# First attention's softmax weights: the multiplication moved to GpSimd, one bounding step on VectorE, one step to bf16 on GpSimd

## The reference, cut to what matters

```python
def _fq(x, delta, zp, n_bits):
    xi = _round_ste(x / delta) + zp
    xq = jnp.clip(xi, 0.0, 2.0 ** n_bits - 1.0)
    return (xq - zp) * delta
...
sim = jnp.einsum('bhid,bhjd->bhij', _fq(q, dq, 128.0, 8), _fq(k, dk, 128.0, 8)) * SCALE
attn = jax.nn.softmax(sim, axis=-1)
out = jnp.einsum('bhij,bhjd->bhid', _fq(attn, dw, 0.0, 8), _fq(v, dv, 128.0, 8))
```

## Time and profile before

| | |
|---|---|
| time, median of 3 runs | 3125.79 us (3118.36 to 3126.36) |
| the profiled execution | 3128.91 us, span 3127.2 us |
| busy: TensorE, VectorE, ScalarE, GpSimd | 2520.2, 1899.8, 1297.8, 1023.1 us |
| mean granted TensorE clock | 0.843 |
| recurrence, about 2512 to 2766 us | 254 us |
| last attention, about 2766 to 3127 us | 361 us |

### The profile page before, as it was taken

The page is one execution under the profiler, slowest core; times in us unless marked ns, Lnnn a source line. Parts: engine busy times, 40 slices in busy tenths (PEclk is TensorE's granted clock), DMA queues, the critical chain, the costliest instruction groups (busy, mean ns, idle before and its releaser), DMA issues. The chain is left out here.

```text
span 3127.2 us, 47208 instructions
## 1 busy us (share of the span) xinstructions
PE 2520.2 (81%) x16568; PEld 1811.3 (58%) x16568; DVE 1899.8 (61%) x4639; ACT 1297.8 (42%) x3243; POOL 1023.1 (33%) x903
## 2 busy tenths in 40 slices
PE   4369888898888888898989898888888765448997
PEld 3247676666666766575767666666666442334443
DVE  4975666776766576868686767676764320004766
ACT  1534344545443345454444544344432211224654
POOL 3841132423242233343333334242321010005775
PEclk9679898898888989898989898979888765558999
DMA  4220011101111011111111111110110000001110
GB/s 187 45 52 10 20 18 24 38 21 21 31 31 24 18 28 31 31 25 27 35 24 29 30 24 28 23 28 22 28 25 7 5 18 23 0 0 34 35 37 22
DMA packets 222407, 90.45 MB, mean 29 GB/s; under 512 B 205280, under 2 KB 212784, under 8 KB 221424
## 3 DMA queue, kind: packets, MB, share of 16 engines
q1 hardware_dynamic: 215728, 67.68, 10.9%
q10 hardware_dynamic: 6464, 19.93, 1.7%
HBM read 27.80 MB, written 9.44 MB: 12 GB/s over the span
## 5 line engine op out<-in xcount | busy, mean ns | idle before, releaser
L775 POOL TENSOR_SCALAR work<-work 128x1024 bf16<-128x1024 f32 x128 | 466.6, 3650 | 319.4 <-DVE work L1285 260.6
L1002 PE MATMUL psum<-hT,w_l 128*128 128x256 f32 x2048 | 490.1, 397 | 19.2 <-ACT hT L1356 9.4
L1002 PEld LDWEIGHTS psum<-hT,w_l 128*128 128x128 f32 x2048 | 401.6, 199 | 90.5 <-ACT hT L1356 14.0
L734 POOL TENSOR_TENSOR rstd<-ms,half 128x2 f32<-128x2 f32 (+1 forms) x144 | 101.5, 706 | 850.1 <-DVE ms L1089 446.1
L1456 ACT ACTIVATE work<-psum 128x1024 f32<-128x1024 f32 (+1 forms) x224 | 222.0, 1021 | 284.9 <-PE psum L934 251.8
L1440 ACT ACTIVATE work<-psum,nbias,qs 128x256 f32<-128x256 f32 x512 | 281.6, 565 | 122.4 <-DVE nbias L1194 120.4
L827 PE MATMUL psum<-hT,w_l 128*128 128x256 f32 x896 | 249.4, 433 | 14.7 <-ACT hT L1356 13.5
L836 PE MATMUL psum<-w_l,xhat 128*128 128x256 f32 x640 | 198.2, 464 | 50.1 <-DVE xhat L1265 34.7
L1014 PE MATMUL psum<-w_l,work 128*128 128x256 f32 x1024 | 231.9, 385 | 2.4 <-DVE work L1318 2.1
L827 PEld LDWEIGHTS psum<-hT,w_l 128*128 128x128 f32 x896 | 189.7, 219 | 58.1 <-issue 18.7
L1356 ACT ACTIVATE hT<-psum,cols 128x256 f32<-128x256 f32 x256 | 121.9, 530 | 230.4 <-PE psum L818 229.3
(11 more groups left out here) (183 smaller groups left out, 4719.7 us busy)
## 6 DMA issues: line engine op xcount, KB each, us to landing
w_l<-in_w_l ACTq DMA_DIRECT2D x1, 5120.0 KB, 25.1
x_res<-in_x SPq DMA_DIRECT2D x16, 256.0 KB, 2.8
res<-x_res ACTq DMA_DIRECT2D x16, 256.0 KB, 2.4
w_l<-res SPq DMA_DIRECT2D x16, 256.0 KB, 2.8
out<-w_l ACTq DMA_DIRECT2D x16, 256.0 KB, 2.0
w_l<-in_w_l ACTq DMA_DIRECT2D x1, 3072.0 KB, 13.4
work<-work SPq DMA_TRANSPOSE x192, 3.1
w_l<-in_w_l SPq DMA_DIRECT2D x2, 1024.0 KB, 8.5
```

What stands on the lines that cost most here:

```text
L775: eng.tensor_scalar(rounded_part(a, u, i, p), e_part(a, u, i, p), MAGIC, -MAGIC, ALU.add, ALU.add) \
L1002: mm = eng.matmul(banks.tile(key)[:, h * TOKENS:(h + 1) * TOKENS], w1[:, k, h, m * P:(m + 1) * P], hT[p][:, k, :], start=(k == 0), stop=(k ...
```

## The change

In A1's rounds, VectorE's `probs` ends with `rsum`. GpSimd's `probs` multiplies the e slot's 4 x 256 columns by the broadcast `rsum`, in place. VectorE's `round_off`, until now only A2's, takes the minimum with 255 and adds MAGIC on all 1024 columns. GpSimd's new `whole` subtracts MAGIC, multiplies by 1.0 and writes bf16. The rounding is done by VectorE's addition of MAGIC now. The transposes, and the exponentials that take the slot again, wait for the new signal `whole_ready`.

The plan is given the new steps and other durations: A1's rounds get 0.6 (VectorE), 2.0 (GpSimd), 0.85 (VectorE), 1.2 (GpSimd) in place of 2.1 and 2.05; A2's rounding 1.15 in place of 1.0. A task can now have a `lag`, a time after its end before its followers start, which leaves its engine free: a transpose holds `sync` for 1.25 us and lands 2.0 later, and loads and stores have a lag of 2.0 in place of tasks on `clock`.

```diff
-TURN, LAND = 2.5, 2.5
+LAND = 2.0
...
-            rest[t] = self.us[t] + max([HOP + rest[f] for f in followers[t]], default=0.0)
+            rest[t] = self.us[t] + self.lag[t] + max([HOP + rest[f] for f in followers[t]], default=0.0)
...
-                    soonest[f] = max(end[b] + HOP * (b[0] != f[0]) for b in self.after[f])
+                    soonest[f] = max(end[b] + self.lag[b] + HOP * (b[0] != f[0]) for b in self.after[f])
...
-                e = work.add("vector", "probs", a, (u, i), p, 2.1 if a.self_attn else 1.4, e)
-                if not a.self_attn:
-                    e = work.add("pool", "probs", a, (u, i), p, 1.25, e)
-                e = work.add("pool" if a.self_attn else "vector", "round", a, (u, i), p, 2.05 if a.self_attn else 1.0, e,
-                             turned.get(2 * u + i - HELD))
+                e = work.add("vector", "probs", a, (u, i), p, 0.6 if a.self_attn else 1.4, e)
+                e = work.add("pool", "probs", a, (u, i), p, 2.0 if a.self_attn else 1.25, e)
+                e = work.add("vector", "round", a, (u, i), p, 0.85 if a.self_attn else 1.15, e,
+                             None if a.self_attn else turned.get(2 * u + i - HELD))
+                if a.self_attn:
+                    e = work.add("pool", "whole", a, (u, i), p, 1.2, e, turned.get(2 * u + i - HELD))
                 rounds[2 * u + i] = e
-                turned[2 * u + i] = work.add("sync", "turn", a, (u, i), p, TURN, e,
-                                             weighed if a.self_attn else None, v if a.self_attn else None)
+                turned[2 * u + i] = work.add("sync", "turn", a, (u, i), p, 1.25, e,
+                                             weighed if a.self_attn else None, v if a.self_attn else None, lag=LAND)
...
-        x = work.add("clock", "stored", None, 0, p, LAND, earlier(p, "scalar", "store", None, 0)) if p >= STREAMS else None
-        x = work.add("sync", "load", "x", 0, p, 0.3, x)
-        x = work.add("clock", "loaded", "x", 0, p, LAND, x)
+        x = work.add("sync", "load", "x", 0, p, 0.3, earlier(p, "scalar", "store", None, 0), lag=LAND)
...
-                    eng.wait_ge(*(probs_ready_p if a is A1 else probs_ready_v).at((a.name, u, i, p)))
+                    eng.wait_ge(*(whole_ready if a is A1 else probs_ready_v).at((a.name, u, i, p)))
...
                 def probs(a, part, p):
                     u, i = part
-                    e = e_part(a, u, i, p).rearrange("p (c n) -> p c n", n=CTX)
+                    heads, n = (4, TOKENS) if a is A1 else (8, CTX)
+                    e = e_part(a, u, i, p).rearrange("p (c n) -> p c n", n=n)
                     eng.wait_ge(*norm_step.at(("p", a.name, u, i, p)))
-                    eng.tensor_tensor(e, e, bcast(rsum[:, stat(p, u, i), :].unsqueeze(2), [P, 8, CTX]), ALU.mult) \
+                    eng.tensor_tensor(e, e, bcast(rsum[:, stat(p, u, i), 0:heads].unsqueeze(2), [P, heads, n]), ALU.mult) \
                         .then_inc(*probs_ready_p.next((a.name, u, i, p)))
 
-                def round_off(a, part, p):
+                def whole(a, part, p):
                     u, i = part
+                    eng.wait_ge(*norm_step.at(("up", a.name, u, i, p)))
                     if 2 * u + i >= HELD:
                         eng.wait_ge(*turned[part_slot(u, i, p)].at((a.name, *before(u, i), p)))
-                    eng.wait_ge(*norm_step.at(("up", a.name, u, i, p)))
-                    eng.tensor_scalar(rounded_part(a, u, i, p), e_part(a, u, i, p), MAGIC, -MAGIC, ALU.add, ALU.add) \
-                        .then_inc(*probs_ready_p.next((a.name, u, i, p)))
+                    eng.tensor_scalar(rounded_part(a, u, i, p), e_part(a, u, i, p), -MAGIC, 1.0, ALU.add, ALU.mult) \
+                        .then_inc(*whole_ready.next((a.name, u, i, p)))
...
-                    if a is A2:
-                        return
-                    eng.wait_ge(*norm_step.at(("p", *key)))
-                    for h in range(4):
-                        e = e_part(a, u, i, p)[:, h * TOKENS:(h + 1) * TOKENS]
-                        ins = eng.tensor_scalar(e, e, rsum[:, r, h:h + 1], 255.0, ALU.mult, ALU.min)
-                    ins.then_inc(*norm_step.next(("up", *key)))
...
                     eng.tensor_scalar(e, e, 255.0, MAGIC, ALU.min, ALU.add).then_inc(*norm_step.next(("up", a.name, u, i, p)))
+                    if a is A1:
+                        return
...
                     if 2 * u + i >= HELD:
-                        eng.wait_ge(*probs_ready_p.at((a.name, *before(u, i), p)))
+                        eng.wait_ge(*whole_ready.at((a.name, *before(u, i), p)))
```

More of the change, by code:

```diff
@@ L79, in __init__, with add @@
     def __init__(self):
-        self.us, self.after, self.fills = {}, {}, {}
-    def add(self, engine, kind, what, part, p, us, *after, fills=()):
+        self.us, self.after, self.fills, self.lag = {}, {}, {}, {}
+    def add(self, engine, kind, what, part, p, us, *after, fills=(), lag=0.0):
         task = (engine, kind, what, part, p)
-        self.us[task], self.after[task], self.fills[task] = us, [t for t in after if t], fills
+        self.us[task], self.after[task], self.fills[task], self.lag[task] = us, [t for t in after if t], fills, lag
         return task
@@ L280, in context_of @@
             before = [earlier(p, "tensor", "context_" + what, MH, 0) for what in ("keys", "values")]
[L281 removed]
+            before = [work.add("sync", "load", "ctx", 0, p, 0.3, *before, lag=LAND)]
             before.append(("scalar", "store", None, 0, p - STREAMS - 1) if p > STREAMS else None)
```

9 lines of the change are left out of this document (4 added, 5 removed).

## The result

The changed kernel takes 3201.94 us in the median (3199.68 to 3210.46), the kernel before 3122.23 in the runs beside it (3118.36 to 3126.36). The ratio is 1.026 [1.0234 to 1.0286]: 80 us slower, where 26 us faster was forecast, and 44 us above the upper end of the range. The profiled execution took 3201.0 us with a span of 3199.3, 72.1 us more than before.

What follows compares the result with a forecast made beforehand. TensorE was taken as nearest its limit (87% busy), idling in many small waits, with GpSimd pacing the start. Start 8, passage 9 and planner 10 us gave -27, so 3100 us from 3125.8; the 8-in-10 range was 3055 to 3158.

Steps and rivals of the forecast that it cites:

- The lengths of the new steps: First attention's rounds: GpSimd multiplication 2.0 us, VectorE min/add 0.68, GpSimd last step 1.2.
- Rival 4: GpSimd's last step isn't faster, running at L775's 3.6 ns a column: 3195 us; chance 0.03.
- The chain of the round: First attention's round, multiplication to last step with three handoffs: 4.2 instead of 4.9 us, 0.7 less.
- the planner's: Truer assumed durations place fewer instructions before their data: 0.8 us an interval gained, 10 us over 13.
- The bound of 154 us in all 12 intervals: Planner term's worst case: if all intervals between elements were 154 us, 44 us would be lost.
- The passage: An element's way through its stream: -3 - 0.5 + 1.5 = -2 us, giving -9 us over 13 intervals.
- The rule of the third: With three streams, one microsecond less in an element's passage gives about a third of one in the interval.
- Rival 2: Hidden: a round's 0.7 us falls into waits the order imposes anyway, only the start gains; 3118 us, chance 0.17.
- The port: GpSimd's two-input steps block VectorE's tensor_scalars 3.2 instead of 1.1 us a round, 17 more an element; charged 1.5 us of passage.
- The added wait: VectorE waits before the min/add for GpSimd's multiplication: under 15 us in all, mostly in idle time; bounds 0 and 256.
- The start: To about 160 us, some 20 rounds paced by GpSimd gain 0.44 us each; 8 us taken.
- Rival 3: Slower, by port and new order: blocked port meets awaited VectorE instructions, 3 us more an interval; near 3155 us, chance 0.25.

Runs made afterwards that it cites:

- e4: Kernel before, own order: VectorE's four steps multiply and add MAGIC, GpSimd takes the minimum with MAGIC + 255 and subtracts MAGIC; 3120.46 us.
- e9: Kernel before, own order: VectorE's four steps multiply and add MAGIC, GpSimd subtracts MAGIC and takes the minimum with 255; 3128.91 us.
- e2: Instructions of the changed kernel in the order of the kernel before, the added steps put in at the times its plan implies; 3144.79 us.
- e1: Instructions of the kernel before, issued in the changed kernel's order on every engine; 3212.14 us.
- e3: Kernel before, instructions unchanged, the plan's assumed duration of the second attention's rounding 1.15 instead of 1.0 us; 3170.74 us.
- e5: Kernel before, own order, bound at 255 left out: VectorE's four steps multiply and add MAGIC, GpSimd subtracts MAGIC and multiplies by 1.0; 3076.74 us.
- e11: e5 plus two unused GpSimd two-input multiplications of 400 columns before each of the 128 last steps; 3139.74 us.
- e12: e5 plus four unused GpSimd memsets of 400 columns before each last step; 3127.64 us.
- e8: Changed kernel, same instructions, planned with the old handling of DMAs, a handoff of 0.1 us and other assumed round durations; 3160.46 us.

## Why the prediction was wrong, point by point

**The lengths of the new steps were right.** The multiplication was put at 2.0 us and takes 1.947 in the mean, the min/add at 0.68 and 0.801 in the mean (0.69 in the median, the rest hold-ups), the last step at 1.2 and 1.083. Rival 4, a slow last step, fell, although e4 and e9 show that it was close by: with the bound in that step it would have been 3.63. (Its price of 3195 us doesn't follow from its own figures: 6 us in each of 13 intervals on top of 3100 are 3178 without the start.)

**The chain of the round failed.** Three handoffs of 0.1 us were to make it 4.2 instead of 4.9 us, 0.7 less. It became 1.1 us longer in the median, 6.09 in e2 and 6.06 in the changed kernel for 4.99. The handoff back to VectorE isn't 0.1 but 1.4 us in the median, since the min/add stands in VectorE's in-order queue behind other work.

**The step that failed most is the planner's.** It was forecast to give 0.8 us an interval, 10 in all, with 44 us of loss as its bound. The reason held as far as it went: the waits of L954 fell from 30.5 to 15.9 us. What was not seen is that the same list moves everything else too. The waits for the normalised rows rose by 64 us, TensorE idled 12 us more a pair of elements, and at the lower clock its matmuls took 12 us longer, 24 in all. The term's true size is a loss of 57 us with the new steps (e2 against the changed kernel) and of 90 with the old (e1). The bound of 154 us in all 12 intervals, 3.7 more than before, was the wrong shape. The first L775 of the tenth and the sixteenth element start at 1317.6 and 2267.6 us in the changed kernel, at 1325.60 and 2215.42 before: by this mark nothing is lost up to the tenth, and from there the intervals are 158.3 us in the mean instead of 148.3. And the range of intervals in one order says nothing of another order: all of the earlier trace rows came from the best of the four orders later seen. Rows of one order don't bound another; e3 shows that even 0.15 us in one constant is worth 48 us.

**The passage.** Besides the chain's wrong sign, the price of a shorter passage was off: a third of it was to come back in each interval. e5 gives 4.0 us an early interval and 1.0 a later one for rounds that are 21 us shorter in all, so a fifth and a twentieth. The rule of the third came from counting streams and wasn't in any row; the even intervals near 147 us in the earlier trace rows already hinted that something else sets them. Rival 2 (hidden) named this mechanism, and fits the late intervals only.

**The port.** The direction was right and the delays are of the size forecast (L1103 and L1101 held up in e2 to 575 and 613 ns in the mean, before 461 and 444). The changed kernel's VectorE lost the 164.7 us for which L1285's group was busy before, gained 102.0, and is busy only 17 us less, so some 46 us more of the rest of its work is hold-up, about 2.9 us an element, besides the 0.11 us in each min/add. The charge of 1.5 us of passage, a third of it an interval, made 6 us. By the half us of e11 and e12 it would be 23 us for 46, an estimate.

One reading behind the charge was incomplete. L775 was said to block the first 1.1 us of its 3.64 and no more. It also blocks about the last one. The L775 of the earlier trace rows ends at 1551.13, and an L1285 that starts under it at 1550.16 takes 1.12 instead of 0.35 us and ends 0.15 after it:

```profile
1550.16 1.12 DVE L1285 TENSOR_SCALAR work<-work,rsum 128x256 f32<-128x256 f32 x1
```

Of the L1285 instructions in the trace of before, all that start 1.1 to 2.5 us after an L775 take 0.35 us, and all that start in its last 1.06 us take 1.03 to 1.20. So about 2.1 us of the old step were blocked, and the new steps (1.9 + 1.0) add 0.8 us a round, some 7 an element, in place of 17.

**The added wait** was put under 15 us, mostly hidden, and is 41.9 us, within its bounds and nearly three times the term; the second attention's two waits in 64 were no guide, though its multiplication has the same form. In e2, with the old order, they are 26.6 us, so the order has a part in it. The term also counted VectorE's idle time alone and not the time that the bounded round stands in VectorE's queue, which is the larger part (see the chain above).

**The start** was to gain 8 us, by GpSimd's 0.44 a round. It gained none. A2's last VectorE step starts first at 161.5 us before and last at 2358.8; in the changed kernel it is 167.7 and 2427.8, and in e2 163.2 and 2380.8. Before and changed:

```profile
L1296 DVE TENSOR_SCALAR work<-work x64: 482/484/1381, 161.5 to 2358.8; 128x616 bf16<-128x616 f32 x64
```

```profile
L1291 DVE TENSOR_SCALAR work<-work x64: 482/484/2055, 167.7 to 2427.8; 128x616 bf16<-128x616 f32 x64
```

Between 60 and 160 us VectorE is busy for 94.2 of 100 us in the changed kernel, GpSimd for 70.6: so GpSimd hardly paces the start any more, and VectorE is as full as before; that hold-ups took what its multiplications gave is argued, not shown. These rows also place the loss: 6 us by 168 us, 63 up to 2428, 3 behind it.

**The rivals.** Rival 3 (slower, by the port and the new order) is what happened, with its 0.25; its price of 3155 was 47 us short. e2 comes near it (3145) with the new steps and no new order, so with the port, the longer round and the added wait together; the order was the larger part and had been let in as a condition, "intervals of 153 us", with no price of its own.

**What stays open.** That the order costs the time is shown; what in it does was not isolated. The plan's simulated end doesn't predict it, and no single wait ranks the orders. How e2's 22 us divide between hold-ups and the longer round is open. Nor is it settled how e5's 45 us divide between the shorter round and the fewer hold-ups: VectorE is busy 34 us less than before, for about 17 us by the price above, which leaves 28 for the round, an estimate.

## What to carry to other kernels

Where a program writes the order from assumed durations, an edit of the tasks is two changes: time the old instructions in the new order and the new instructions in the old order before judging either, and be ready for the order to be the larger (here 57 to 90 us against 10 to 22) and not to get better because a duration got truer. Moving work to an engine with idle time is paid twice on the engine that it leaves: in hold-ups, so compare the busy time of that engine's unchanged instructions before and after; and in the way back, which costs what stands ahead in that engine's queue (here 1.4 us in the median) and not the handoff of 0.1. The gain here lay in the pair of operations that GpSimd runs fast, with the multiplications left where they were.

## What the runs showed of the hardware

- GpSimd's tensor_scalar of 128x1024, f32 to bf16, takes 1.04 us with (add, mult) and 3.63 with (add, add), (min, add) or (add, min).
- The (add, add) form blocks VectorE's tensor_scalars of SBUF data in about its first 1.1 us and its last one, not between: an L1285 that starts between them takes 0.35 us, one that starts in the last stretch 1.03 to 1.20.
- A GpSimd memset holds up VectorE's tensor_scalars too: with four of 432 ns (median) a round, a 256-column instruction goes from 351 to 453 ns in the mean.
- The clock can double the price of waits, and need not. In a pair of elements of the changed kernel 12 us more of idle time came with 12 us more for the same matmuls, at 0.86 instead of 0.89; over the whole span TensorE's busy time rose by 19 of the 72 us. In e8 (span 3158.1 us, 30.9 more than before) TensorE's busy time rose by 24.0 us for the same 16568 matmuls (2544.2 for 2520.2) and its idle time by 7. In e11 TensorE is idle for 256 us from 412 to 2300, 18 more than before, at 0.89:

```profile
412.00:2300.00 1888.00, 1631.63 (x11370) 1220.92 (x11369) 1374.24 (x3171) 846.91 (x1830) 544.91 (x621) 0.89 0.13 27
```
